# A fused attention and feed-forward kernel: heads of P normalised one by one, and another order of the work in a unit, at the K to Q seam and between the phases

## What is computed

```python
# 8 batches of 128 tokens, D = 512; 32 heads of 128
h = layernorm(x); xq = rmsnorm(h) * ln_weight
q, k, v = xq @ w_q.T, ctx @ w_k.T, ctx @ w_v.T
score = q . k per head + position_bias, masked keys at -inf
P = softmax(score), 0 where masked
attn_out = h + (P @ v) @ w_out.T
x = x + tanh(g_xattn) * attn_out
y = layernorm(x)
ffn = y @ base_W.T + base_b + routed LoRA (15 router outputs, 8 experts of rank 16)
out = x + tanh(g_ffn) * ffn
```

## Time and profile before

| What | Value |
|---|---|
| Time before, median of 3 runs | 880.85 us (877.19 to 882.0) |
| The profiled execution, its own time | 884.0 us |
| Its span | 882.1 us |
| PE busy | 844.8 us (96%) |
| DVE busy | 675.5 us (77%) |
| ACT busy | 499.0 us (57%) |
| POOL busy | 489.1 us (55%) |

### The profile page before, as it was taken

One profiled execution on the slowest core, in us unless ns is written; L12 is line 12 of the kernel. 1 busy time (PEld: TensorE's weight loads), 2 busy tenths in 40 slices (PEclk: granted clock), 3 DMA queues, 4 the chain that ended last, 5 costly groups with the idle time before them and its releaser, 6 DMA issues.

```text
span 882.1 us, 13849 instructions
## 1 busy us (share of the span) xinstructions
PE 844.8 (96%) x4204; PEld 707.1 (80%) x4204; DVE 675.5 (77%) x1174; ACT 499.0 (57%) x1185; POOL 489.1 (55%) x352
## 2 busy tenths in 40 slices
PE   6999999989999996899999999999999999998898
PEld 5887888778888885788888888888888888877786
DVE  6888777886765645788788888888888888899764
ACT  5566676666676644555655655555555556554410
POOL 0353534644466523666666766666666666656432
PEclk9999999999999998999999999999999999998999
DMA  8876677679777787888888888888888888985101
GB/s 288 306 274 246 251 286 266 225 281 368 281 284 278 271 311 228 251 238 256 250 241 261 248 256 244 252 251 246 237 252 244 233 251 248 273 270 161 35 25 72
DMA packets 155392, 214.72 MB, mean 243 GB/s; under 512 B 10960, under 2 KB 109392, under 8 KB 154960
## 3 DMA queue, kind: packets, MB, share of 16 engines
q1 hardware_dynamic: 155344, 214.13, 75.8%
HBM read 128.11 MB, written 85.98 MB: 243 GB/s over the span
## 4 chain that ended last, share of the span: by engine, by line
DVE 40%; PE 34%; ACT 12%; issue 7%; DMA 5%; SPq 1%; DVEq 1%; POOL 0%; ACTq 0%
ACT p_exp L746 10%; DVE p_norm L1080 5%; PE Sb L1353 5%; PE Sb L1355 4%; PE Sb L1354 4%; DVE s_sb L1063 4%; DVE rscale L1075 4%; DVE negmax L1065 4%; DVE s_sb L1061 4%; DVE V_lo L910 4%; DVE acc L1095 3%; DMA pT<-p_rows 2%; PE Ab L1353 2%; PE Ab L1355 2%; PE Ab L1354 2%
## 5 line engine op out<-in xcount | busy, mean ns | idle before, releaser
L474 POOL TENSOR_TENSOR w_lo<-w_raw,w_hi 128x1280 fp32r<-128x1280 f32 (+1 forms) x29 | 84.8, 2924 | 121.5 <-ACT w_hi L612 121.5
L518 POOL TENSOR_TENSOR a_rest<-small_a,A_hi 128x512 f32<-128x512 f32 x64 | 84.1, 1313 | 82.3 <-ACT small_a L740 82.3
L746 ACT ACTIVATE p_exp<-s_sb,negmax 128x128 f32<-128x128 f32 x256 | 99.7, 391 | 52.6 <-DVE negmax L1065 52.4
L523 POOL TENSOR_TENSOR P_hl<-pT,P_hl 128x512 fp32r<-128x512 f32 x64 | 82.7, 1293 | 78.3 <-ACT P_hl L612 78.2
L612 ACT ACTIVATE P_hl<-pT 128x512 fp32r<-128x512 f32 x64 | 40.5, 633 | 117.7 <-DMA pT<-p_rows 117.7
L511 POOL TENSOR_TENSOR bm<-bias,maskneg 128x512 f32<-128x512 f32 x64 | 83.1, 1299 | 24.3 <-DVE s_sb L1061 24.3
L1513 PE MATMUL Ab<-P_hl,V_hi 128*128 128x256 f32 x256 | 66.5, 337 | 20.4 <-POOL P_hl L523 10.7
L612 ACT ACTIVATE U<-Sb 128x512 f32<-128x512 f32 x90 | 53.7, 600 | 41.5 <-PE Sb L1355 40.9
L1513 PEld LDWEIGHTS Ab<-P_hl,V_hi 128*128 128x128 f32 x256 | 49.1, 192 | 34.0 <-POOL P_hl L523 20.4
L612 ACT ACTIVATE w_hi<-w_raw 128x512 fp32r<-128x512 f32 (+2 forms) x67 | 60.2, 903 | 22.7 <-PE Kb L1355 6.9
L1353 PE MATMUL Sb<-t_hi,w_lo 128*128 128x512 f32 x180 | 70.3, 391 | 2.2 <-ACT U L612 2.2
(11 more groups left out here) (300 smaller groups left out, 2755.6 us busy)
## 6 DMA issues: line engine op xcount, KB each, us to landing
qk_units<-unit_out SPq DMA_DIRECT2D x128, 512.0 KB, 3.1
qk<-qk_units SPq DMA_DIRECT2D x64, 1024.0 KB, 7.3
p_rows<-p_blocks SPq DMA_DIRECT2D x64, 256.0 KB, 2.8
pT<-p_rows SPq DMA_DIRECT2D x256, 64.0 KB, 4.3
w_raw<-wqk SPq DMA_DIRECT2D x31, 512.0 KB, 4.3
v_raw<-wv SPq DMA_DIRECT2D x32, 256.0 KB, 4.9
o_raw<-wo SPq DMA_DIRECT2D x32, 256.0 KB, 4.8
stage<-ctxT SPq DMA_DIRECT2D x8, 256.0 KB, 6.4
```

Of the source, the lines that this page charges most:

```text
L474: pool.tensor_tensor(w_lo[:, n % 2, first:5, :], w_raw[:, n % 2, first:5, :], f32(w_hi[:, n % 2, first:5, :]), ALU.subtract).then_inc(w1_l ...
L518: pool.tensor_tensor(a_rest[:, :, :], small_a[:, :, :], f32(A_hi[:, r, :, :]), ALU.subtract).then_inc(a_rest_done, 1)
L523: pool.tensor_tensor(blocked(P_hl[:, :, 1, :]), queries(pT[:, r, :, :, :]), f32(blocked(P_hl[:, :, 0, :])), ALU.subtract).then_inc(p_lo_do ...
L746: last = act.activation(p_exp[:, i, :], s_sb[:, i, :], ACT.Exp, bias=negmax[:, i:i + 1], accum_out=rowsum[:, i:i + 1])
```

## The change

1. `normalise` loses the product `rscale = rinv * valid` and the one product over 512 elements. In their place stand four `tensor_scalar` operations of 128 elements, one per head, each of which multiplies by two per-row numbers, `rinv` of the head and `valid` of the batch.
2. In every unit DVE runs `scores`, `attention_lo`, `v_evict_lo`, `add_out` (before: `add_out`, `v_evict_lo`, `scores`, `attention_lo`). ACT copies `small_attention` ahead of `v_evict_hi`. The loads and splits of the next group's weights come two units later.
3. At the K to Q seam ACT runs `c12_hi(15)` after, not before, the snapshots `snapshot_3(16)` and `snapshot_1(17)`.
4. Between the phases: the scores of units 0 and 1 go to bank QP by three matmuls of 128 columns a head (`scores_early`), unit 0 in the middle of the last job, unit 1 before V of unit 0. Their maxima, exponentials, normalisation and transposition move along. SP stores the last three results of job 31 only in steps 4 to 6, and issues the first units' loads in a new order (`first_units`). V of unit 1 is made in Kb. The store of P's blocks is one run of 2 KB per row.
5. Buffers are laid out in another order, so that `s_sb`, `p_exp` and `p_norm` are free before the first phase ends.

```diff
@@ SP
-                sp.dma_start(p_rows[b % 2, :, :, :],
-                             p_blocks[:, :, :, :].rearrange("p j h r -> p j (h r)")).then_inc(rows_done, 16)
+                sp.dma_start(p_rows[b % 2, :, :, :].rearrange("p j n -> p (j n)"),
+                             p_blocks[:, :, :, :].rearrange("p j h r -> p (j h r)")).then_inc(rows_done, 16)
...
+            def first_units():
+                for i in range(4):
+                    sp.wait_ge(st[i], 16 * (G + 2))
+                sp.wait_ge(scores_done, 1)
+                load_unit(0, 2)
+                store_blocks(0, 0)
+                load_blocks(0, 0)
+                sp.wait_ge(scores_done, 2)
+                load_unit(0, 3)
...
@@ ACT, step
-                if not (first and b == 0):
-                    v_evict_hi(t, b)
-                if not (first and b < 3):
-                    small_attention(t - 3)
...
+                small_attention(t - 3)
+                v_evict_hi(t, b)
...
@@ ACT, jobs
                 snapshot_1(n)
+                if n == G + 1:
+                    c12_hi(G - 1)
...
-                if n > PLAIN:
+                if n > PLAIN and n != G and n < JOBS - 1:
                     c12_hi(n - 1)
+                if n == JOBS - 1:
+                    exponentials(0)
...
@@ ACT, between the phases
+            probs_hi(0, 0, 1)
+            exponentials(2)
+            v_evict_hi(1, 1)
+            v_evict_hi(2, 2)
+            attention_hi(0, 0)
+            small_attention(0)
+            v_evict_hi(3, 3)
...
@@ DVE
-                dve.tensor_tensor(rscale[:, :], rinv[:, :], valid[:, b:b + 1].broadcast_to([P, HU]),
-                                  ALU.mult).then_inc(rscale_done, 1)
-                dve.wait_ge(rscale_done, u + 1)
                 reached(dve, blocks_done, u)
-                scale = rscale[:, :].rearrange("p (b o) -> p b o", o=1).broadcast_to([P, HU, S])
-                dve.tensor_tensor(p_norm[:, :, :], p_exp[:, :, :], scale, ALU.mult).then_inc(norm_done, 1)
+                for h in range(HU):
+                    last = dve.tensor_scalar(p_norm[:, h, :], p_exp[:, h, :], rinv[:, h:h + 1], valid[:, b:b + 1],
+                                             ALU.mult, ALU.mult)
+                last.then_inc(norm_done, 1)
...
@@ DVE, step
+                scores(t)
+                attention_lo(t - 3, (b - 3) % 2)
+                v_evict_lo(t, b)
                 if last and b >= 5:
                     x1(b - 5)
                     x1_stats(b - 5)
                 elif not (first and b < 5):
                     add_out(t - 5, (b - 5) % B)
-                if not (first and b == 0):
-                    v_evict_lo(t, b)
-                scores(t)
-                if not (first and b < 3):
-                    attention_lo(t - 3, (b - 3) % 2)
...
@@ PE
+            def scores_early(u):
+                pe.wait_ge(ld_qk[u % 2], 16)
+                reached(pe, first_sum_done, u)
+                for h in range(HU):
+                    K_hl, Q_hl = qk[:, u % 2, h, 0, :], qk[:, u % 2, h, 1, :]
+                    pe.matmul(QP[:, tok(h)], Q_hl[:, S:2 * S], K_hl[:, 0:S], start=True, stop=False)
+                    pe.matmul(QP[:, tok(h)], Q_hl[:, 0:S], K_hl[:, S:2 * S], start=False, stop=False)
+                    last = pe.matmul(QP[:, tok(h)], Q_hl[:, 0:S], K_hl[:, 0:S], start=False, stop=True)
+                last.then_inc(scores_done, 1)
...
                 if n > PLAIN:
                     m4(n - 1)
+                if n == JOBS - 1:
+                    m3(n - 1)
+                    scores_early(0)
                 m6(n)
...
+            scores_early(1)
             v_half(0, 0, 0, 0, 0)
             m4(JOBS - 1)
             v_half(0, 0, 0, 0, 1)
-            v_half(1, 0, 1, 0, 0)
-            scores(0, 0, 0)
             m3(JOBS - 1)
-            v_half(1, 0, 1, 0, 1)
-            for b in range(1, B):
+            scores(2, 0, 2)
+            for b in (1, 2):
+                v_half(b, 0, b, 0, 0)
+                v_half(b, 0, b, 0, 1)
+            apply_probs(0, 0)
+            v_half(3, 0, 3, 0, 0)
+            v_half(3, 0, 3, 0, 1)
+            for b in range(3, B):
                 step(0, b, 0)
```

More of the change, by code:

```diff
@@ L402, in _ @@
                     store(R12, n - 1)
+            def first_units():
[7 more added lines that the diff above has]
+                load_unit(0, 3)
+                store_blocks(0, 1)
+                load_blocks(0, 1)
+                sp.wait_ge(scores_done, 3)
+                load_unit(0, 4)
+                store_blocks(0, 2)
+                load_blocks(0, 2)
+                sp.wait_ge(m_done[4], J(JOBS - 1))
+                load_wv(1, 1, 0)
+                sp.wait_ge(scores_done, 4)
+                load_unit(0, 5)
+                load_wv(1, 1, 1)
             def group(g, q):
                 first, last = (isinstance(g, int) and g == n for n in (0, GROUPS - 1))
-                for b in range(B):
-                    if first and b == 0:
-                        for i in range(4):
-                            sp.wait_ge(st[i], 16 * (G + 2))
-                    if first and b == 4:
+                for b in range(4 if first else 0, B):
+                    if first and b == 7:
                         for i in range(4):
@@ L418, in group @@
                         load_unit(g + (b + 2) // B, (b + 2) % B)
-                    if not (first and b == 0):
-                        load_blocks(*before)
-                    if first and b == 0:
-                        sp.wait_ge(m_done[4], J(JOBS - 1))
-                    if b < DC and not last:
-                        load_wv(g + 1, 1 - q, b)
-                    if b == 1 and not last:
+                    load_blocks(*before)
+                    if 2 <= b <= 5 and not last:
+                        load_wv(g + 1, 1 - q, b - 2)
+                    if b >= 6 and not last:
+                        load_wo(g + 1, 1 - q, b - 6)
+                    if b < 2 and not first:
+                        load_wo(g, q, b + 2)
+                    if b == (4 if first else 1) and not last:
                         load_bias(g + 1, 1 - q)
-                    if b >= DC and not last:
-                        load_wo(g + 1, 1 - q, b - DC)
+                    if first and b > 3 and b < 7:
+                        store((R22, R21, R12)[b - 4], JOBS - 1)
                     if last and b == 0:
@@ L538, in step @@
                 first, last = (isinstance(g, int) and g == n for n in (0, GROUPS - 1))
-                if not (first and b < 3):
-                    a_remainder(t - 3, (b - 3) % 2)
-                if not (first and b < 2):
-                    probs_lo(t - 2, b % 2)
+                a_remainder(t - 3, (b - 3) % 2)
+                probs_lo(t - 2, b % 2)
                 if last and b >= 5:
@@ L579, in _ @@
             bias_and_mask(0, 0, 0)
-            for b in range(B):
+            bias_and_mask(0, 1, 0)
+            bias_and_mask(0, 2, 0)
+            bias_and_mask(0, 3, 0)
+            probs_lo(0, 0)
+            a_remainder(0, 0)
+            probs_lo(1, 1)
+            bias_and_mask(0, 4, 0)
+            split_wv_lo(1, 1, 0)
+            for b in range(4, B):
                 step(0, b, 0)
@@ L825, in _ @@
                     c21_hi(n - 1)
+                    exponentials(1)
                     v_evict_hi(0, 0)
@@ L865, in _ @@
                     hidden(n - G - 1)
-            for b in range(B):
+            probs_hi(0, 0, 1)
[5 more added lines that the diff above has]
+            v_evict_hi(3, 3)
+            probs_hi(1, 1, 1)
+            exponentials(3)
+            split_wv_hi(1, 1, 0)
+            for b in range(4, B):
                 step(0, b, 0)
@@ L1245, in _ @@
                     router_constants()
-            for b in range(B):
+            v_evict_lo(1, 1)
+            normalise(2, 2)
+            transpose_blocks(2)
+            v_evict_lo(2, 2)
+            attention_lo(0, 0)
+            scores(3)
+            v_evict_lo(3, 3)
+            normalise(3, 3)
+            transpose_blocks(3)
+            for b in range(4, B):
                 step(0, b, 0)
```

92 lines of the change are left out of this document (54 added, 38 removed).

## The result

The changed kernel takes 913.87 us (median of 4 runs, 909.34 to 915.6) where the kernel before takes 879.02 (4 runs beside them): a ratio of 1.0377, 95% interval 1.0339 to 1.0415. It is some 33 us slower, and 60 us above the forecast of 854.

What follows compares the result with a forecast made beforehand. PE was taken as the bound (96% busy), losing time between phases, in short loop stops and at the end. Gains 13 + 0.5 + 10 + 3.5 = 27 us from the profiled 884.0, less 3.15 to the median, give 854; range 847 to 867.

Steps and rivals of the forecast that it cites:

- PE covers it: Normalisation in the loop: DVE's 0.25 us less per unit is worth nothing by itself, because PE's work hides it.
- K to Q: Phase change in projections: snapshots go first, their 2.16 us wait goes, POOL's weights are late next; 0.5 us won, bounds 0 to 2.2.
- Normalisation: Four operations replacing two in each unit: 1.09 us in the clear, 0.25 us less on DVE, no gain in total.
- The rival: Four normalisation operations lose the port to POOL, up to 1.3 us each; loop step 7.96 us, total 891; chance 0.05.
- The order in a unit: Loop: A_lo and P leave DVE earlier, ending PE's short waits; 10 of 12.4 us gained, bounds 0 and 12.4.
- Between the phases: Before the attention loop: earlier P of unit 0 removes PE's pauses except one of 1.9 us; 13 us gained, bounds 8 to 15.8.
- The rival on SP's chain: Between the phases: P of unit 0 or a Q/K load comes late through SP's strict chain, 8 us stay; 859 to 862, chance 0.13.
- End of the loop: Last units: PE's waits of 2.65 and 2.29 us for A_lo shorten; 3.5 us gained, bounds 0 and 8.
- the sign of being wrong: DVE's loop idle time gone and PE waiting for A_lo or P in most steps, or a pause over 4 us between phases.
- the chance of 0.62: Probability given to the forecast itself, for a time of 846 to 860 us.

Runs made afterwards that it cites:

- the queue mended: Changed kernel with one normalisation operation and tiles on old addresses, plus SP's weights load and P-block stores moved ahead of what delayed them: 865.07 us, ratio 0.9801.

## Why the prediction was wrong, step by step

The step that failed is the one on the normalisation: it put the four operations at nothing, since "PE covers it". They cost 33 us against the two operations of before and 36 against one, because each of their gaps lets one queued operation of POOL in front.

From 1.0377 down, the runs give the 60 us a place: the four operations 0.0412 of the ratio (36 us), the tiles' places 0.0038 (3, uncertain), SP's queue 0.0126 (11). From 0.9801 to the forecast, 854 / 880.85 = 0.9695, 0.0106 (9) is left, and this is a balance: K to Q and the seam gave 7.6 us where 13.5 were forecast, the 13.5 for the order and the end show in no run's time, and the one operation gave 10 that the forecast did not have. The order of this ladder matters: behind the four the seam's 11 us are hidden.

- *Normalisation* (0 forecast): the step that failed. The duration in the clear was right (1.11 for 1.09). What failed is "PE covers it". The rival had the mechanism, one turn of up to 1.3 us at each gap, two of them in every other unit, and nearly its price: steps of 7.80 us in the loop (405.63 / 52) for 7.96. I gave it 0.05 because POOL has 2 us a step with nothing to do. That is a mean. POOL's mask sum and the split behind it run when the exponentials do, so the queue is full exactly when DVE comes to the four (POOL at 664.35, 665.58 and 666.84, DVE at 665.34). And its 891 kept the seam's gain and charged the end nothing; there three operations are queued, 4.07 us, and 11.2 us went.
- *The order in a unit* (−10): the mechanism was half right, the gain is not in the time. The waits for A_lo go as forecast, but P's normalisation comes to lie under POOL's work, which the forecast did not follow. The median shows nothing, in either kernel. One operation for the normalisation takes 9 of the loop's us in either order.
- *Between the phases* (−13): the mechanism was right (the pause before V of unit 2, forecast 1.9 us, is 1.54; P of unit 0 no longer waits), but SP's queue was followed to unit 2 and no further. The rival on SP's chain had the place; it expected 8 us to stay, and nothing did. With the queue mended, the seam of 0.9801 against 0.9887 (before with one operation) shows 7.6 us, K to Q and the later weights included, for 13.5.
- *K to Q* (−0.5): right in size: 0.41 and 1.21 us of waits instead of 2.16. Wrong in what is late next: of the two, at 185.61 and 189.78, the first is for DVE and the second still for ACT's snapshot, neither for POOL's weights.
- *End of the loop* (−3.5): wrong sign, +11.2. From unit 62 to the end it is 83.2 us before, 85.1 with the new order alone, 84.1 in the change with the pair of before, and 94.4 with the four: some 10 of the 11.2 are the four, and without them the gain is missing all the same. The step of DVE there was put at 8.7 us without the turns it loses.
- What I named as the sign of being wrong is what came: DVE's idle time gone in half of the units (25 of 49), a wait of PE of over 0.1 us in 32 of the 52 steps (17 of the waits for P or A_lo), and a pause of over 4 us at the seam (4.49).
- The sums hold, but for the chance of 0.62: it is given to 846 to 860, and the range stated is 847 to 867.
- The Trainium skill, "VectorE: DVE Perf Modes", section on the TRN2 errata, advises against small pieces for their fixed latency. Its advice was right, and the latency is there: 1.11 us in the clear for four, 0.55 for one of the same form. The larger part of the price is not latency but up to three turns.

## What to carry to other kernels

Where VectorE and GpSimd both work from SBUF, count the gaps inside a block of small operations, and look at what GpSimd has queued at that moment, not at its mean load: a gap costs up to one GpSimd operation (1.3 us here). Put such work in one operation, or hold GpSimd's until it is through. When work is moved across a queue, follow that queue until every load that stood behind it has been taken. And when a small tile goes, see whether the tiles behind it move: here that made the loop's step 1% longer.

## What the runs showed of the hardware

VectorE and GpSimd take turns by instruction: of back-to-back blocks in SBUF, one operation of VectorE, then one of GpSimd, each at its full length, so that four pieces of 1.11 us together stretch to 3.14 against two operations of 1.3 and to 4.07 against three. What reads an operand from PSUM (A_lo, 0.68 us) loses no turn. And moving the tiles by 32 bytes, with no instruction changed, lengthens a step of the loop from 7.32 to 7.42 us.
